# Up weights fetched from HBM for each tile of tokens, into a ring of eight, in place of sixteen kept experts and an on-chip copy

## What is computed

```python
h = einsum('bnf,ef->bne', patches(x), W) + b
h = h + attention(layernorm(h))
t = rmsnorm(layernorm(h));  g = t @ gate_w.T + gate_b
top_vals, top_idx = top_k(g, 4);  route_w = softmax(top_vals)
up   = t @ mlp1_w[e].T + mlp1_b[e]        # 192 -> 2*384
a    = min(glu, 7) * sigmoid(1.702 * glu) * (clip(lin, -7, 7) + 1)
y    = a @ mlp2_w[e].T + mlp2_b[e]        # 384 -> 192
out  = h + layernorm(h) + sum over the token's 4 experts of route_w * y
```

## Time and profile before

| | |
|---|---|
| three runs, median (range) | 290.84 us (290.64 to 290.85) |
| the profiled execution: time | 291.94 us |
| its span in the trace | 290.2 us |
| mean granted TensorE clock | 0.934 |
| PE busy | 256.5 us, 88% |
| POOL, DVE, ACT busy | 172.6, 168.7, 113.3 us |
| moved by DMA | 31.29 MB |

### The profile page before, as it was taken

The page is one execution under the profiler, slowest core; times in us unless marked ns, Lnnn a source line. Parts: engine busy times, 40 slices in busy tenths (PEclk is TensorE's granted clock), DMA queues, the critical chain, the costliest instruction groups (busy, mean ns, idle before and its releaser), DMA issues.

```text
span 290.2 us, 6337 instructions
## 1 busy us (share of the span) xinstructions
PE 256.5 (88%) x1943; PEld 249.8 (86%) x1943; DVE 168.7 (58%) x425; ACT 113.3 (39%) x291; POOL 172.6 (59%) x202
## 2 busy tenths in 40 slices
PE   2899999997577079999999999999999999999980
PEld 1799999986456079999999999999999999999970
DVE  0014465567897117676676766767766667676640
ACT  1010212233142125545554555455455545554520
POOL 5013266668897412567776666767766666665752
PEclk9999999999655559999999999999999999999996
DMA  6998999999812993323423243422322333233100
GB/s 180 232 216 201 235 229 232 270 278 282 241 16 58 259 244 105 48 34 56 62 49 47 45 58 54 59 42 31 50 47 49 51 49 56 32 43 52 19 1 0
DMA packets 18589, 31.29 MB, mean 108 GB/s; under 512 B 5629, under 2 KB 12125, under 8 KB 18557
## 3 DMA queue, kind: packets, MB, share of 16 engines
q1 hardware_dynamic: 7862, 22.33, 31.2%
q0 software_dynamic: 8640, 7.76, 17.6%
q10 hardware_dynamic: 2055, 0.80, 1.1%
HBM read 26.39 MB, written 5.96 MB: 111 GB/s over the span
## 4 chain that ended last, share of the span: by engine, by line
PE 78%; DMA 9%; POOL 5%; issue 2%; DVE 2%; POOLq 1%; SPq 1%; ACT 1%; DVEq 0%
PE bank L1098 39%; PE bank L1107 14%; PE bank L905 11%; DMA hn_all<-t_rows,get_row 4%; PE bank L1080 3%; DMA x_sb<-in_x 3%; PE bank L1048 2%; PE bank L934 2%; PE bank L942 2%; DMA out<-hn_all,put_row 2%; PE bank L951 1%; POOL ln_all L429 1%; PE bank L914 1%; PE bank L1067 1%; POOL rstd L422 1%
## 5 line engine op out<-in xcount | busy, mean ns | idle before, releaser
L1098 PE MATMUL bank<-xT,x_sb 96*128 96x128 f32 (+1 forms) x1080 | 136.9, 276 | 0.8 <-ACT xT L594 0.8
L1098 PEld LDWEIGHTS bank<-xT,x_sb 96*128 96x128 f32 (+1 forms) x1080 | 131.6, 193 | 1.2 <-issue 1.2
L481 POOL DMA_INDIRECT out<-hn_all,put_row x45 | 73.0, 1622 | 52.5 <-issue 23.2
L465 POOL DMA_INDIRECT hn_all<-t_rows,get_row x45 | 47.2, 1049 | 21.0 <-issue 12.5
L1107 PE MATMUL bank<-w_sb,tokw 128*128 x270 | 51.4, 326 | 0.7 <-DVE tokw L880 0.7
L1107 PEld LDWEIGHTS bank<-w_sb,tokw 128*128 128x128 f32 x270 | 42.9, 190 | 1.0 <-issue 1.0
L869 DVE TENSOR_SCALAR ln_all<-bank 128x384 f32<-128x384 f32 x45 | 25.1, 558 | 31.4 <-PE bank L1098 31.4
L905 PE MATMUL bank<-tokw,x_sb 120*120 120x192 f32 x192 | 37.0, 353 | 6.8 <-DMA x_sb<-in_x 6.8
L611 ACT COPY x_sb<-w_sb 96x768 f32 x45 | 37.0, 823 | 12.4 <-PEq L1090 10.3
L905 PEld LDWEIGHTS bank<-tokw,x_sb 120*120 120x120 f32 x192 | 34.2, 199 | 7.8 <-DMA x_sb<-in_x 7.8
L873 DVE TENSOR_TENSOR ln_all<-ln_all 128x384 f32<-128x384 f32 x45 | 25.2, 560 | 26.5 <-ACT ln_all L630 26.5
(11 more groups left out here) (143 smaller groups left out, 229.4 us busy)
## 6 DMA issues: line engine op xcount, KB each, us to landing
w_sb<-in_w SPq DMA_DIRECT2D x16, 576.0 KB, 14.8
x_sb<-in_x SPq DMA_DIRECT2D x7, 675.0 KB, 10.9
w_sb<-in_w SPq DMA_DIRECT2D x16, 288.0 KB, 15.9
t_rows<-hn_all ACTq DMA_DIRECT2D x8, 90.0 KB, 7.9
out<-h SPq DMA_DIRECT2D x1, 720.0 KB, 6.1
hn_all<-t_rows,get_row POOLq DMA_INDIRECT x45, 3.2
out<-hn_all,put_row POOLq DMA_INDIRECT x45, 3.5
tokw<-in_tok_w SPq DMA_DIRECT2D x1, 540.0 KB, 6.7
```

The source lines that it names most:

```text
L465: g.indirect_dma_start(out=xg[slot], out_offset=None, in_=t_rows, in_offset=bass.IndirectOffsetOnAxis(ap=get_row[:, m:m + 1], axis=0),).th ...
L481: g.indirect_dma_start(out=out, out_offset=bass.IndirectOffsetOnAxis(ap=put_row[:, m:m + 1], axis=0), in_=ysb[m % RING], in_offset=None, c ...
L1098: ins = t.matmul(dst[:, m * SLOTS:(m + 1) * SLOTS], stage[0:rows, j % 2, c, o:o + 128], xT[0:rows, j % 2, c, :], start=(c == 0), stop=(c = ...
```

## The change

The up weights are no longer kept. SP's front loads only the sixteen w2, four behind each of x[4] to x[7]. When `owner` is known, SP loads w1 and the b1 row of tile j's owner into place j mod 8 of a ring, with an address from a register. Tiles 0 and 1 go out at once. Ahead of tile 2 stands the base store, and ahead of that the waits for `s_b2c` and for the first two gathers. From tile 8 on a load waits until up(j-8,1) has read its place. PE reads the ring itself; `stage`, both copies, `here` and `s_ready` are gone.

```diff
-SETTLED = 12
-HELD = 4
+WRING = 8
...
-        w1_sb = sb("w1_sb", [128, E * W1E])
+        w1_sb = sb("w1_sb", [128, WRING * W1E])
...
-        stage = x_sb[0:HK + 1, 0:2 * W1E].rearrange("p (b c n) -> p b c n", b=2, c=HC)
+        w1_ring = w1_sb[0:HK + 1, :].rearrange("p (b c n) -> p b c n", b=WRING, c=HC)
...
-            def load_expert(e):
-                sp.dma_start(w1_sb[0:HK, e * W1E:(e + 1) * W1E], w1[e]).then_inc(s_w[e], 16)
-                sp.dma_start(w2_sb[:, e * W2E:(e + 1) * W2E], w2[e]).then_inc(s_w[e], 16)
+            def load_down(e):
+                sp.dma_start(w2_sb[:, e * W2E:(e + 1) * W2E], w2[e]).then_inc(s_w2, 16)
...
-                if i == RING:
-                    sp.dma_start(w1_sb[HK:HK + 1, :].rearrange("p (e c n) -> p e c n", e=E, c=HC)[:, :, HC - 1, :],
-                                 b1).then_inc(s_b1, 16)
-
                 if i > RING:
-                    load_expert(i - RING - 1)
-            for e in range(TILES - RING - 1, E):
-                if e == E - HELD:
+                    for e in range(4 * (i - RING - 1), 4 * (i - RING)):
+                        load_down(e)
+
+
+            sp.wait_ge(s_owner, 1)
+            experts = []
+            for j in range(MT):
+                if j % GROUP == 0:
+                    experts.extend(owners(mybir.EngineType.SP, j // GROUP))
+                if j == 2:
 
                     sp.wait_ge(s_b2c, 4)
+                    for m in range(2):
+                        sp.wait_ge(s_got[m], 16)
                     sp.dma_start(out[0:TOKENS, :].rearrange("(i p) n -> p i n", p=TT), h[:, :, :]).then_inc(s_base_out, 16)
-                load_expert(e)
-
-
-            for e in range(E):
-                sp.wait_ge(s_w[e], 32)
-                sp.sem_inc(s_ready, 1)
+                if j >= WRING:
+                    sp.wait_ge(s_lin, j - WRING + 1)
+                b = j % WRING
+                sp.dma_start(w1_sb[0:HK, b * W1E:(b + 1) * W1E],
+                             w1[bass.ds(experts[j], 1)].rearrange("a p n -> (a p) n")).then_inc(s_w1[b], 16)
+                sp.dma_start(w1_sb[HK:HK + 1, b * W1E + 2 * I:(b + 1) * W1E],
+                             b1[:, bass.ds(experts[j], 1), :].rearrange("a e n -> (a e) n")).then_inc(s_w1[b], 16)
...
             def copy_weight(j):
+                if j % GROUP == 0:
+                    experts.extend(owners(mybir.EngineType.Activation, j // GROUP))
...
-                a.copy(stage[0:HK, j % 2, 0, :], w1_sb[0:HK, bass.ds(experts[j] * W1E, 2 * I)]).then_inc(s_stage_0, 1)
...
-            stage_half(0)
             copy_xT(0)
             copy_weight(0)
             for j in range(MT):
-                if j + 1 < MT:
-                    stage_half(j + 1)
...
-              d.tensor_copy(stage[:, j % 2, 1, :],
-                              w1_sb[0:HK + 1, bass.ds(experts[j] * W1E + 2 * I, 2 * I)]).then_inc(s_stage_1, 1)
...
-            pe.wait_ge(s_b1, 16)
...
-                        ins = t.matmul(dst[:, m * SLOTS:(m + 1) * SLOTS], stage[0:rows, j % 2, c, o:o + 128],
+                        ins = t.matmul(dst[:, m * SLOTS:(m + 1) * SLOTS], w1_ring[0:rows, j % WRING, c, o:o + 128],
...
-            here(0)
-            here(1)
...
-                if j + 2 < MT:
-                    here(j + 2)
-                pe.wait_ge(s_stage_0, j + 1)
-                pe.wait_ge(s_stage_1, j + 1)
+                pe.wait_ge(s_w1[j % WRING], 32 * (j // WRING + 1))
...
                 if j >= 1:
+                    if j == 1:
+                        pe.wait_ge(s_w2, 16 * E)
                     down(j - 1)
```

More of the change, by code:

```diff
@@ L213, in audio_tower_kernel @@
         s_qkvw = sem("s_qkvw")
-        s_b1 = sem("s_b1")
-        s_w = [sem(f"s_w{e}") for e in range(E)]
-        s_ready = sem("s_ready")
+        s_w1 = [sem(f"s_w1_{b}") for b in range(WRING)]
+        s_w2 = sem("s_w2")
         N_SMALL = 5
@@ L303, in audio_tower_kernel @@
         s_a = sem("s_a")
-        s_here = sem("s_here")
-        s_stage_0 = sem("s_stage_0")
-        s_stage_1 = sem("s_stage_1")
         s_y = sem("s_y")
@@ L1081, in turn_x @@
                 ins.then_inc(s_xT, 1)
[L1083 to L1090, removed]
             def up(j, part, dst):
```

## The result

The changed kernel takes **313.43 us** (median, 310.26 to 316.60), the kernel before 290.85. The ratio is 1.074 (95% interval 1.062 to 1.086): the medians are 22.6 us apart, where 9.2 was forecast. The direction and the range (286 to 314) held, the size did not. The profiled execution took 312.29 us with a span of 310.4 us, 20.2 more than before.

What follows compares the result with a forecast made beforehand. The prediction took PE as the bound of the steady expert loop, DMA of the front, POOL close behind. Its terms -4.6 + 12 + 2 gave +9.4 us on 290.84, so 300.2 us, range 286 to 314.

Steps and rivals of the forecast that it cites:

- Part 1: Start of the expert stage: first gather lands earlier, turn_x(0) at 97.8 instead of 102.38, a gain of 4.6 us.
- Part 2: Front: four w2 behind each x add 1.2 us of loads, but cost nothing; 1.2 us if the cover fell.
- Part 3: Loads after the start: full queue delays gathers and scatters, PE waits at tiles 5 to 7, a loss of 12 us.
- Part 4: Rest of the loop: loads may delay scatters at changes of owner, 0 to +31 us, taken as +2.
- Clock: Start of the expert stage: PE clock at its lower level, 1.2 GHz, in either kernel, so no difference counted.
- Taking turns: DMA engines serve queues in turn, delaying small transfers 2.4 us, sum about +3; set aside for the traced 5.6 us.
- rival 2: DMA engines become the second bound to the end of the loop: 318 us, or 309 with half; chance 0.14.

Runs made afterwards that it cites:

- kept_hold_paced: Kernel before, with base store and last four experts held until two gathers land, those experts issued one after another, first twelve counted earlier: 294.57 us, ratio 1.013.
- stop8: Changed kernel with no up weights loaded from tile 8 on, so those tiles use wrong weights: 292.45 us (one time).
- lead3: Changed kernel with at most three up-weight loads in the queue, all bytes still moved: 303.85 us.
- half8: Changed kernel with each up-weight load from tile 8 on bringing only half the columns, so weights are wrong: 294.27 us (one time).
- two_targets: Changed kernel with odd tiles' scatters going to a second tensor and no wait for the scatter just before; output incomplete: 297.04 us, ratio 1.017.
- kept_spread: kept_hold_paced with the four held experts' w1 loaded at s_lin 5 to 8 and w2 at 9 to 12, one at a time: 292.65 us, ratio 0.996.
- kept_spread2: kept_hold_paced with the four held experts' w1 loaded at s_lin 8 to 11 and w2 at 15, 16, 19 and 20: 285.84 us, ratio 0.980.
- late_phase: Changed kernel with every up-weight load from tile 8 on issued 2.3 us later in the tile: 308.75 us (one time).
- nob1: Changed kernel with bias rows loaded for the first eight tiles only, leaving out 37 small loads: 308.14 us (one time).
- nohold: Changed kernel without the wait for two gathers ahead of the base store and the loads from tile 2 on: 306.36 us (one time).

## Why the prediction was right in direction and wrong in size

- **Part 1, the start: right.** Forecast -4.6 (3.4 to 5.8); the ledger has -5.39, then -4.65. The first gather took 3.8 us. What I wrote of the first copies ("their removal is needed for this gain") is not so once SP counts the kept experts ahead of the hold: `kept_hold_paced` has the gain with its copies. Two runs isolate the reason: without the hold it is -0.19, and with the hold and all copies -6.49. PE reached the upper clock later in its work (the next 24 passes of up took 4.50 us against 3.48); 0.7 us of the gain was lost by tile 3, which I had counted as none.
- **Part 2, the front: right.** No wait of the front grew; `owner` is written at 88.65 against 88.92.
- **Part 3, the waits at tiles 5 to 8: right.** Forecast 12 (10.0 to 15.6), measured 14.5. The way was right (PE waits for gathers behind waiting scatters), the single prices only in their sum: 5.3, 3.4 and 3.4 us at tiles 5 to 7 where I had 3.2, 6.2 and 0.6 to 6.2, and 2.5 at tile 8, where I had none. scatter(0) landed in 11.9 us, not 9.1, and scatter(1) in 7.7. The DMA engines were less full than I had it: share 1.02 to 120 us, but 0.73 from 120 to 140. What I had argued from depth is only partly depth: stop8 leaves 5.9, lead3 6.4. A single load under a scatter that is waited for costs 2 to 3 us.
- **Part 4, the rest of the loop: wrong, this is the step that failed.** I wrote "+31 us at most, and 0 at least" and took **+2**, because "most of the load is over when the scatter's rows move". It measured +11.3. (My count of 19 other tiles is 17 up to tile 40, which makes the upper bound +32.) The size of the collision, 6.85 us from scatter to scatter, was right for the worst (6.74, 7.25, 7.47). What failed is the step from the time between load and scatter to a small term. I looked at the load issued ahead of the scatter, which does little; the one that delays it is the next, issued behind it. And I took a scatter that keeps time. The first scatter of a new owner does not: its ordinary wait (4.4 to 4.8 us from start to start against the pace of 3.87) brings it so near the next load that this one is issued 1.0 to 1.3 us behind it, and tiles 12, 20 and 27 landed in 5.7 to 6.0 us. That is free where the next scatter has the same owner (12, 27) and costs 2.9 us where it has another (tile 20, alone in its run: 6.74 us to scatter(21)). The lateness that is left, caught up at 0.58 us per tile, does the same to the second scatter of a short run (28, in 6.46 us). Such short runs, of 1, 2, 2, 2 and 2 tiles, begin at tile 20. half8 shows that the size of the load is needed, two_targets that the wait is. kept_spread and kept_spread2 show that a long landing costs nothing where nobody waits for it. late_phase says that another place for all loads does not change the sum by much, and which part of the 11 us lies in which collision stays open. It also varies: 11.3, 7.6 (`nob1`) and 5.8 us (`nohold`, behind tile 10) in three kernels with nearly the same loop, so that a part of 11.3 may be chance of one execution.
- **Clock.** PE's stalls lowered the granted clock for a while each (0.911 on the mean against 0.934); the busy time of the up products is 142.8 us against 136.9. I had counted none.
- **Taking turns.** The Trainium skill (DMA: Bandwidth & Descriptors, Queues, rings and completion order) has each DMA engine take its queues in turn. By it the sum would have been about +3. With the prediction's estimate of 2.4 us for the delay, a scatter would land in 5.9 us. Landings of 4.7 to 6.8 us beside single loads agree with that; 9.8 to 11.9 us under the full queue do not, and these make more than half of the early waits. Why a landing grows further there no run here shows.
- **Of the rivals**, the bound by the DMA engines (rival 2, 309 to 318) gave the right time by luck in the main: the later loss is half of its 20 us and sits in two places, not at every change of owner, and between 180 and 200 us the engines run at 0.86 and PE loses nothing.

## What to carry to other kernels

When loads are moved beside small transfers, ask for each small one who waits for its landing. A landing that nobody waits for may double for free; one in a chain (here scatter after scatter) has to be priced by the late case, with the lateness carried on from one wait to the next, and not by the case in which everything keeps time. And a gain at the head of a stage (5.4 us by letting two gathers go first) can be taken alone: with the kept weights it makes the kernel 2% faster, if the delayed loads are put where no landing is waited for.

## What the runs showed of the hardware

- A scatter of an occupied tile lands in 2.9 to 3.8 us in the kernel before (four of 40 in 4.1 to 4.6). Beside one 576 KB load it depends on the place: 5.2 to 6.5 us when the load is issued 0.6 to 1.5 us behind the scatter's start, 3.1 to 4.4 us for nearly all when it is issued 1.75 us behind or later. With half the load (`half8`) 1.1 to 1.4 us behind, five landed in 4.5 to 5.1 us and one in 6.3.
- Behind the base store and six to eight loads issued in about 12 us ahead, scatter(0) landed in 11.9 us (the changed kernel), 10.7 (`half8`), 9.8 (`stop8`) and 11.1 us (`two_targets`).
- SP issues a load with an address from a register in 0.32 us (median), up to 1.44 us at the start of the stage; one with a fixed address took 0.39 to 1.68 us in the kernel before, 0.31 in `kept_hold_paced`.
- The median of the scatters' landings hides all this: 3.7 us against 3.5.
